# Roots of the first norms moved from GpSimd to ScalarE and VectorE, beside GpSimd's gathers

## The reference

```python
xn = _layernorm(x, axis=-1)            # (x - m) / sqrt(v + 1e-5)
feat_src = (sent_repr @ W_src).reshape(NS, H, DH)
er = jnp.sum((word_repr @ W_dst).reshape(NW, H, DH) * attn_r, axis=-1)   # word_repr = xn
# per edge: leaky_relu(el[src] + er[dst]), a softmax over the edges of each dst,
# and the weighted sum of feat_src[src] over 53125 edges
qkv = jnp.einsum('bld,df->blf', xn, W_qkv)   # first mixer
```

## Time and profile before

| what | us |
|---|---|
| median of 3 runs | 2205.79 (2203.96 to 2211.80) |
| the profiled execution | 2211.77 |
| its span | 2210.10 |
| TensorE busy | 1599.5 (72%) |
| VectorE busy | 1250.0 (57%) |
| GpSimd busy | 1068.4 (48%) |
| ScalarE busy | 874.0 (40%) |

### The profile page before, as it was taken

One profiled execution on the slowest core, in us unless ns is written; L12 is line 12 of the kernel. 1 busy time (PEld: TensorE's weight loads), 2 busy tenths in 40 slices (PEclk: granted clock), 3 DMA queues, 4 the chain that ended last, 5 costly groups with the idle time before them and its releaser, 6 DMA issues. The chain is left out here.

```text
span 2210.1 us, 31483 instructions
## 1 busy us (share of the span) xinstructions
PE 1599.5 (72%) x7770; PEld 1248.9 (57%) x7770; DVE 1250.0 (57%) x3879; ACT 874.0 (40%) x2979; POOL 1068.4 (48%) x1173
## 2 busy tenths in 40 slices
PE   5535677666766676969999766776787776974792
PEld 4533444444444445959999654555565555763792
DVE  3523655556556587855777634554555554675435
ACT  2221655665656586645777421000011000153451
POOL 2751666666666500421222256666666666225341
PEclk8665677777777797989999777888888888995896
DMA  5741544444444302836555232333333333122786
GB/s 188 218 141 38 152 121 123 125 133 123 129 128 126 98 18 73 264 109 203 181 165 179 73 99 84 89 91 90 88 90 89 88 91 93 42 87 80 219 263 222
DMA packets 176882, 276.92 MB, mean 125 GB/s; under 512 B 28920, under 2 KB 132218, under 8 KB 176456
## 3 DMA queue, kind: packets, MB, share of 16 engines
q0 software_dynamic: 50352, 136.58, 21.5%
q1 hardware_dynamic: 82194, 94.23, 14.0%
q10 hardware_dynamic: 44166, 44.14, 6.0%
HBM read 202.35 MB, written 73.58 MB: 125 GB/s over the span
## 5 line engine op out<-in xcount | busy, mean ns | idle before, releaser
L501 POOL DMA_INDIRECT ring<-feat_d,src_lane x440 | 433.0, 984 | 282.9 <-issue 121.5
L1221 POOL DMA_INDIRECT rows<-xn_d,src_of x416 | 404.2, 972 | 236.3 <-issue 106.0
L1201 PE MATMUL bank<-ring,a_hot 128*128 128x260 f32 x880 | 319.0, 511 | 147.9 <-DVE ring L1100 64.7
L1392 PE MATMUL bank<-rows,big 128*128 x880 | 288.9, 445 | 138.8 <-DVE big L1300 66.7
L1130 ACT ACTIVATE ring<-ring 128x64 f32<-128x64 f32 x1540 | 376.7, 336 | 15.8 <-issue 14.8
L1201 PEld LDWEIGHTS bank<-ring,a_hot 128*128 128x128 f32 x880 | 204.8, 251 | 226.0 <-DVE ring L1100 83.6
L1309 DVE TENSOR_TENSOR big<-bank,big 128x256 f32 x440 | 186.6, 424 | 233.4 <-DMA m_bo<-in_L_mix_bo 112.1
L1392 PEld LDWEIGHTS bank<-rows,big 128*128 128x128 f32 x880 | 165.6, 211 | 236.7 <-issue 222.1
L1085 DVE TENSOR_TENSOR acc<-bank,acc 128x260 f32 x440 | 186.8, 425 | 145.9 <-PE bank L1201 59.4
L1362 ACT ACTIVATE big<-bank,a_col 128x256 f32<-128x256 f32 (+1 forms) x26 | 13.1, 553 | 417.4 <-issue 257.2
L1300 DVE TENSOR_SCALAR big<-const,dst_lane,ew_lane 128x128 f32<-128x128 f32 x440 | 151.8, 346 | 1.0 <-PEq L95 1.0
(11 more groups left out here) (405 smaller groups left out, 2901.4 us busy)
## 6 DMA issues: line engine op xcount, KB each, us to landing
slots_d<-fold ACTq DMA_DIRECT2D x25, 1300.0 KB, 5.6
e_w_now<-in_L_ffn_w SPq DMA_DIRECT2D x56, 256.0 KB
a_dst_bc<-dst_lo_d SPq DMA_DIRECT2D x23, 512.0 KB
big<-in_L_ffn_W SPq DMA_DIRECT2D x16, 512.0 KB
e_x<-slots_d SPq DMA_DIRECT2D x56, 130.0 KB
ring<-feat_d,src_lane POOLq DMA_INDIRECT x440
rows<-xn_d,src_of POOLq DMA_INDIRECT x416
e_ys<-y_d SPq DMA_DIRECT2D x24, 256.0 KB
```

The costliest lines, as they stand in the source:

```text
L501: pool.indirect_dma_start(ring[:, q % RING, at, :], None, table, bass.IndirectOffsetOnAxis(ap=src_lane[:, n:n + 1], axis=0)).then_inc(gath ...
L1201: pe.matmul(bank[n % BANKS][:, 0:D + H], hot[:, q % HOTS, at, :], ring[:, q % RING, at, :], start=True, stop=True)\
L1221: pool.indirect_dma_start(rows[:, n % RING1, :], None, table, bass.IndirectOffsetOnAxis(ap=src_of[:, n:n + 1], axis=0)).then_inc(gathered[ ...
L1392: pe.matmul(bank[n % 4][:, 0:D], hot[:, n % HOTS, :], tile_of(rows, slots[n % 4]), start=True, stop=True)\
```

## The change

The five roots leave GpSimd. ScalarE takes the square root of a group's variances (`root`): the first ahead of its first copy, root i + 1 ahead of the copy of tile 5i + 3. VectorE takes the reciprocal ahead of the first tile of each group that it applies, and waits for it through a new semaphore, `inverted`. GpSimd issues 46 gathers in this stage in one run instead of 39 in six, and the next stage's 42 follow, so `BY_THEN` becomes 88 instead of 81.

```diff
--- before.py
+++ after.py
@@ -56,8 +56,8 @@
 DECAY_AT = {start: H * sum(size + 1 for _, size in BLOCKS[:n]) for n, (start, _) in enumerate(BLOCKS)}
 DECAYS = H * sum(size + 1 for _, size in BLOCKS)
 XC = P + H
-EARLY = [0, 4] + [13 + 6 * i for i in range(NI - 1)] + [15 + 6 * (NI - 1)]
-BY_THEN = EARLY[NI + 1] + 42
+EARLY = 46
+BY_THEN = EARLY + 42
 AHEAD = 2 * R
 UP_FIRST = 2 * MAXB // UP
 RING1 = 48
@@ -525,12 +525,12 @@
         x_in = late[:, 0:AHEAD * D].rearrange("p (j n) -> p j n", j=AHEAD)
         xn, xnT = (late[:, AHEAD * D + n * R * D:AHEAD * D + (n + 1) * R * D].rearrange("p (j n) -> p j n", j=R) for n in range(2))
         stats, mv, rstd = sb("p1_stats", [P, AHEAD, 6]), sb("p1_mv", [P, AHEAD, 2]), sb("p1_rstd", [P, AHEAD, 1])
-        power = const[:, C_POW:C_POW + 1]
+        std = sb("p1_std", [P, AHEAD, 1])
         turned_ps, v_ps, k_ps = ([bank[2 * n], bank[2 * n + 1]] for n in range(3))
 
         w_in, wd, w_ready = sem("p1_w_in"), sem("p1_wd"), sem("p1_w_ready")
         x_loaded = [sem(f"p1_x_loaded{j}") for j in range(AHEAD)]
-        measured, averaged, found, rooted = (sem(f"p1_{n}") for n in ("measured", "averaged", "found", "rooted"))
+        measured, averaged, found, rooted, inverted = (sem(f"p1_{n}") for n in ("measured", "averaged", "found", "rooted", "inverted"))
         xn_stored = [sem(f"p1_xn_stored{j}") for j in range(R)]
         xnT_stored = [sem(f"p1_xnT_stored{j}") for j in range(R)]
 
@@ -561,14 +561,8 @@
 
         @block.gpsimd
         def _(pool):
-            for i in range(NI + 1):
-                for n in range(EARLY[i], EARLY[i + 1]):
-                    gather_rows(pool, ring, gathered, src_lane, feat_d, n)
-                if i < NI:
-                    at = i * R % AHEAD
-                    pool.wait_ge(found, i + 1)
-                    pool.tensor_tensor(rstd[:, at:at + R, 0], mv[:, at:at + R, 1], power.broadcast_to([P, R]), ALU.pow)\
-                        .then_inc(rooted, 1)
+            for n in range(EARLY):
+                gather_rows(pool, ring, gathered, src_lane, feat_d, n)
 
         @block.scalar
         def _(act):
@@ -577,8 +571,17 @@
             act.dma_start(w_v[:, :, 0:HD], weights(A["L0_mix_W_v"])).then_inc(w_in, 16)
             act.dma_start(w_k[:, :, :], weights(A["L0_mix_W_k"])).then_inc(w_in, 16)
 
+            def root(i):
+                at = i * R % AHEAD
+                act.wait_ge(found, i + 1)
+                act.activation(std[:, at:at + R, 0], mv[:, at:at + R, 1], ACT.Sqrt).then_inc(rooted, 1)
+
             def copy_xn(i, j):
                 g = i * R + j
+                if g == 0:
+                    root(0)
+                if j == 3 and i + 1 < NI:
+                    root(i + 1)
                 act.wait_ge(turned, g + 1)
                 once(act, k_done, g - R + 1)
                 once(act, xnT_stored[j], i * 16)
@@ -626,7 +629,10 @@
             def apply(g):
                 k = g % AHEAD
                 dve.wait_ge(found, g // R + 1)
-                dve.wait_ge(rooted, g // R + 1)
+                if g % R == 0:
+                    dve.wait_ge(rooted, g // R + 1)
+                    dve.reciprocal(rstd[:, k:k + R, 0], std[:, k:k + R, 0]).then_inc(inverted, 1)
+                dve.wait_ge(inverted, g // R + 1)
                 once(dve, turned, g - R + 1)
                 once(dve, xn_stored[g % R], g // R * 16)
                 dve.tensor_scalar(xn[:, g % R, :], x_in[:, k, :], mv[:, k, 0:1], rstd[:, k, 0:1], ALU.subtract, ALU.mult)\
@@ -731,7 +737,7 @@
 
         @block.gpsimd
         def _(pool):
-            for n in range(EARLY[NI + 1], BY_THEN):
+            for n in range(EARLY, BY_THEN):
                 gather_rows(pool, ring, gathered, src_lane, feat_d, n)
 
         @block.vector
```

## The result

The changed kernel took 2211.23 us in the median of 20 runs (2204.37 to 2224.85), the kernel before 2204.18 us in 20 runs beside it (2187.98 to 2217.38). The ratio is 1.0044 with a 95% interval of 1.0025 to 1.0063: 9.7 us slower (5.5 to 13.9), where 2.7 us faster was forecast. The profiled execution took 2221.67 us (span 2220.0), 9.9 us more than that of before (2211.77).

A forecast was written before the change was run, and what follows sets the result against it. It took TensorE's signals, late while GpSimd issues gathers, as the projections' bound. Terms -0.3 - 0.7 + 0.3 + 1 - 3 = -2.7 us gave 2209.1 us for an execution like the profiled one, 2203.1 for a median; range 2188 to 2219.

The forecast's parts named there:

- What bounds the stage: Projections' stage: TensorE's signals reach other engines late while GpSimd issues gathers; no single engine's work bounds it.
- Roots off GpSimd: Projections' stage: first group's root sooner, -0.3 us; second and later groups, -0.7; roots queued ahead of ScalarE's copies, +0.3.
- if it is done earlier: First group's root: ScalarE's table load runs before the wait, so the root is ready at 57.3 us, not 58.6.
- 46 gathers in a row: Projections' stage: one run ends near 105.3 us, without pauses for held signals; +1 us, between -2.5 and +3.6.
- Both ends: Bounds of the unbroken run's term: copies at 3.75 us a tile give -2.5 us, at 9.1 us a tile +3.6.
- Seven gathers moved ahead: Aggregation: its first run falls from 15 gathers to 8, so it gains 3 us (0 to -3.4).
- Starvation: Rival, chance 0.20: the long run lets nothing through in the projections' stage from 78 to 109.8 us; +14, total 2217 us.
- a gap of over 15 us without a copy: Profile sign in the projections' stage that would show the forecast wrong and the long run starving the stage.
- The roots were the limit: Rival, chance 0.14: late signals only a profile effect; projections' 25 tiles done near 87 us, stage -19 us, total 2184.
- the last rival: Rival, chance 0.06: ScalarE's wait for `found` holds its copies, roots as late as before, total near 2208 us.

The follow-up runs named there:

- m1: Changed kernel with 39 gathers in the earlier six runs, waits between, plus a landing wait after every fourth mixer gather; late: 2179.08 us against 2205.80, ratio 0.9892.
- c0: The kernel before, unchanged, profiled once more; late condition, 2200.46 us.
- e5: The kernel before with a wait for landing after every fourth of the mixer's 42 gathers; prompt condition, ratio 1.0127.
- f5: First repeat of e5, the same kernel; prompt condition, ratio 1.0135.
- g5: Second repeat of e5, the same kernel; prompt condition, ratio 1.0126.
- e1: Changed kernel with the earlier six runs of 39 gathers, GpSimd only waiting for VectorE's statistics between them; prompt: 1898.45 us against 1900.28, ratio 0.9991.
- c1: The changed kernel, unchanged, timed again; late condition, 2216.19 us against 2204.26 for the kernel before, ratio 1.0047.
- h1: The changed kernel, unchanged, timed once more; prompt condition, 1898.13 us against 1901.18 for the kernel before, ratio 0.9992.
- e2: Changed kernel with 39 gathers instead of 46 in its one run, seven back in the aggregation; prompt condition, ratio 0.9982.
- g1: Second repeat of e1, the same kernel; prompt condition, ratio 0.9983.
- q1: Changed kernel with a landing wait after every fourth gather of the projections' and mixer's stages; late: 2195.87 us against 2203.95, ratio 0.9961.

## Why the prediction was wrong

*What bounds the stage*: right for the late condition, in which the traces of the case were taken. The bound is the late signals, not the roots; m1 moves the stage's end by 21 us against the changed kernel with the same roots. Too narrow was "TensorE's signals": VectorE's wait for its own took 5.85 us.

*Roots off GpSimd* (-0.3, -0.7, +0.3): in the changed kernel itself neither gain came. In the first group VectorE applied the root 2.4 us after it had the variances, against 2.2 before: ScalarE's root was ready sooner, but VectorE had other work in between. The second group's variances were there at 62.74, and ScalarE took their root only at 71.70, behind a copy that was itself held; before, the root had ended at 71.42. The first table load ran at 48.34, ahead of the wait, and was hidden as in the case "if it is done earlier"; a square root of 128x5 took 0.21 us, not 0.29. What the step gives where breaks are kept is seen from m1 against before, from the stage's first gather to the next stage's: 75.2 us against 78.3 and 78.4 (c0), so some -3 where -0.7 was summed. That idle breaks let more through than breaks filled by a root is my reading of it and was not tested alone. In the prompt condition the stage takes 61.0 to 62.5 us in e5, f5 and g5, which have the roots on GpSimd, and 56.7 to 59.6 in e1 and its repeats: -4 there.

*46 gathers in a row* (+1, ends -2.5 and +3.6) is **the step that failed**: the stage's end measured +15.6 and, in c1 against c0, +15.4 (by the stage's own length +16.5 and +16.2). Both ends supposed that signals trickle for as long as the run lasts, and I said so. The pace of 3.75 us a tile was that of a stage with breaks, which is what the change removes; the 9.1 us a tile came from the first third of the mixer's run. The row of the whole run stood beside it: no copy from 157 us to 183. The unbroken run of 46 lets four copies through and no more. Of 25 that leaves 21 for the time after the run: 137.31 - 111.64 = 25.7 us from the first of them to the last, 1.28 us each. And the first came 7.1 us after the run (6.7 in c1), where both ends had 1.7.

*Seven gathers moved ahead* (-3, 0 to -3.4): measured -2.6 in the profiled pair (634.1 to 631.5 us). In c0 and c1 it is 625.9 and 625.2, so -0.7. The first cycle, from the aggregation's first gather to the one behind its first wait, is 2.7 us shorter in both pairs (21.8 to 19.1 us); in c0 and c1 most of that is lost again further on. Sign right, size within the bounds given.

*The rivals.* Starvation, at 0.20, is what happened, with the sign it named (a gap of over 15 us without a copy; it was 26.36): it forecast a start between 134.9 and 147.1 (141.9 measured), +14 for the stage (+15.6) and 2217 us, +11 against the median (+9.7 measured). It had 7 copies by 78 us; there were 3. The argument against it, only 5.43 us of standstill in this stage, held for runs of nine gathers and said nothing of 46. "The roots were the limit" failed here, and its 25 tiles without held signals are what h1 does: done at 95.5 us, later than its 87, with the DMA engines busy for 0.98 of the time. Of the last rival one part came true: the second group's root was as late as before, though through the held copy ahead of it and not through the wait for `found`. As for the Trainium skill, "TensorE: Matmul & The Clock Gate", section "The cost: per-tile semaphore tail", with 26.3 ns for each increment: in e2 (prompt) a copy that had only to wait for its transposition started 0.03 to 0.04 us after that ended, so nothing there speaks against the rule; in the late condition it is out by 34 to 37 us.

*The total* was within the range (2188 to 2219) and on the wrong side of no change. That it lay within is owed to the starvation rival, for which the range had been widened, and not to the forecast, whose own range ended at 2211. Of the chances, 0.60 on a term whose two bounds came from one assumption was the error: the bounds were not bounds.

## What to carry over

Read how far a term's bounds share an assumption: a pace taken from a stage with pauses says nothing of one without. Where other engines' signals come late beside a long run of GpSimd's gathers, the pauses in that run are part of the kernel's timing, and only pauses that leave GpSimd idle count; but put them where GpSimd isn't the bound: the waits in the mixer's stage that saved 16.8 us in m1 cost 1.3%, some 24 us, in e5. A version should be timed in both conditions before it is kept: here the change costs 0.44% in one and nothing in the other.

## What the runs showed of the hardware that I had not expected

- One kernel, two times: 1900 and 2204 us, with the same durations of single instructions on GpSimd, ScalarE and VectorE. The difference of some 300 us is waiting, but for some 46 us of TensorE's busy time. Up to the last addition of the aggregation h1 takes 655.5 us and the changed kernel 867.7, so 212 us of it lie there; in the aggregation alone h1 needs 500 us and the changed kernel 631.5.
- In the late condition a signal of TensorE took effect up to 37 us after the matmul, beside a run of gathers 0.30 us apart and for 7.1 us behind it, though nothing in the trace was at work from 106 to 111 us; VectorE's wait for its own signal took up to 5.85 us. In the prompt one, beside the same run, it was 0.04 and 0.03 us.
- An idle stretch of GpSimd of 3.0 to 5.4 us behind four gathers was enough to keep the 25 copies of q1 within 1.8 us of their transpositions. Whether less is enough, whether the idle GpSimd or the landing of its gathers does it, and whether a plain load holds signals too, stays open.
- What puts a chip in one condition or the other stays open; the chip that had the number 14 was prompt for g1 and late for q1, though the number may stand for another machine. The granted clock differs (0.81 and 0.87 in the mean), but so does TensorE's work: in the window from 59 to 97 us it is 0.54 with TensorE busy for 7.45 us, and 0.97 in h1's with 29.86, so it can be a result as well as a cause.
